# Spreading the decays of a state-space scan over the partitions: through memory with broadcast loads instead of TensorE transposes, and the block off the diagonal as a product with a cumulative product

## The reference

```python
xBC = jax.nn.silu(xBC_c.transpose(0, 2, 1) + conv_b)
...
dt = jax.nn.softplus(dt + dt_bias)
A = -jnp.exp(A_log)
...
decay = jnp.exp(dt * A)
dtx = dt[..., None] * xh

def step(h, inp):
    dec_t, dtx_t, B_t, C_t = inp
    h = dec_t[:, :, None, None] * h + dtx_t[..., None] * B_t[:, None, None, :]
    y_t = jnp.einsum('bhpn,bn->bhp', h, C_t)
    return (h, y_t)
```

## Time and profile before

| | us |
|---|---|
| median of 3 runs | 1030.62 |
| lowest, highest | 1022.71, 1031.51 |
| the profiled execution | 1024.98 |
| its span, first to last instruction | 1023.1 |
| mean granted clock of TensorE, as a share of 2.4 GHz | 0.945 |
| a full step of the first stage, steps 4 to 15 | 30.0 to 30.4 |

### The profile page before, as it was taken

How to read it: one execution, slowest core, us unless ns; L and a number is a source line. 1 busy time by engine, 2 the same in 40 slices (tenths; PEclk the granted TensorE clock), 3 DMA queues, 4 the chain that set the end, 5 groups by cost and what they waited for, 6 DMA issues and landing times.

```text
span 1023.1 us, 22359 instructions
## 1 busy us (share of the span) xinstructions
PE 905.9 (89%) x6324; PEld 790.4 (77%) x6325; DVE 724.6 (71%) x2092; ACT 502.3 (49%) x1259; POOL 587.5 (57%) x649
## 2 busy tenths in 40 slices
PE   4697999999999999999874369999999998669998
PEld 3576877877877787887654269999999998558887
DVE  5357799888889989888874335555555554599993
ACT  3333555554555555555322125555555554555653
POOL 5435455777778777777646454444444444365551
PEclk9989999999999999999966679999999999879999
DMA  7400000110100110000095112232221221224332
GB/s 180 90 11 11 1 11 12 31 31 22 30 17 27 32 31 27 16 19 16 18 275 158 40 44 68 78 85 67 65 67 55 58 64 54 56 81 114 97 101 51
DMA packets 72057, 59.12 MB, mean 58 GB/s; under 512 B 19169, under 2 KB 61468, under 8 KB 71985
## 3 DMA queue, kind: packets, MB, share of 16 engines
q1 hardware_dynamic: 63440, 41.88, 15.9%
q0 software_dynamic: 8544, 16.34, 4.8%
HBM read 35.62 MB, written 23.81 MB: 58 GB/s over the span
## 4 chain that ended last, share of the span: by engine, by line
PE 48%; DVE 24%; issue 15%; POOL 8%; another core or an unknown queue 1%; ACT 1%; DMA 1%; SPq 0%; DVEq 0%; POOLq 0%; ACTq 0%
PE psum L967 13%; PE psum L952 13%; DVE arena L1504 4%; DVE arena L1852 4%; PE psum L650 3%; POOL x_slots L1362 3%; PE psum L651 3%; PE psum L652 3%; PE psum L785 2%; PE psum L802 2%; DVE h_all L1552 2%; DVE arena L1857 2%; PE psum L961 2%; POOL arena L1338 2%; DVE arena L1512 2%
## 5 line engine op out<-in xcount | busy, mean ns | idle before, releaser
L1189 ACT ACTIVATE arena<-psum,arena 128x128 f32<-128x128 f32 x556 | 159.0, 369 | 155.9 <-PE psum L952 131.9
L1395 POOL DMA_INDIRECT y_tokens<-arena x139 | 136.8, 984 | 161.0 <-DVE arena L1802 117.1
L952 PE MATMUL psum<-arena 128*128 128x128 f32 x1112 | 154.5, 283 | 27.2 <-DVE arena L1795 15.7
L952 PEld LDWEIGHTS psum<-arena 128*128 128x128 f32 x1112 | 139.9, 198 | 29.1 <-DVE arena L1789 15.3
L967 PE MATMUL psum<-arena 128*128 x1112 | 156.4, 284 | 0.4 <-issue 0.4
L1362 POOL DMA_INDIRECT x_slots<-arena,idx x128 | 128.0, 1000 | 34.6 <-issue 34.3
L967 PEld LDWEIGHTS psum<-arena 128*128 128x128 f32 x1112 | 137.6, 194 | 7.4 <-issue 0.6
L1789 DVE COPY arena<-arena 128x644 f32 x139 | 75.4, 542 | 72.1 <-issue 65.6
L1795 DVE TENSOR_SCALAR arena<-psum,lng,lnb 128x128 f32<-128x128 f32 x139 | 56.9, 409 | 52.5 <-PE psum L961 40.8
L1504 DVE TENSOR_TENSOR_SCAN arena<-psum,arena 124x496 f32<-124x496 f32 x64 | 72.5, 1175 | 11.9 <-PE psum L785 7.8
L1332 POOL TENSOR_TENSOR arena<-arena 128x496 f32<-128x496 f32 x32 | 40.0, 1251 | 34.6 <-DVE arena L1532 34.6
(11 more groups left out here) (283 smaller groups left out, 2215.8 us busy)
## 6 DMA issues: line engine op xcount, KB each, us to landing
arena<-x_slots SPq DMA_DIRECT2D x139, 64.5 KB
arena<-y_tokens SPq DMA_DIRECT2D x16, 448.0 KB
arena<-in_x SPq DMA_DIRECT2D x16, 256.0 KB, 3.2
out_tokens<-arena SPq DMA_DIRECT2D x16, 224.0 KB
y_tokens<-arena POOLq DMA_INDIRECT x139
x_slots<-zero_src SPq DMA_DIRECT2D x33, 64.5 KB, 4.2
moe_all<-in_x SPq DMA_DIRECT2D x4, 512.0 KB, 5.8
x_slots<-arena,idx POOLq DMA_INDIRECT x128
```

The source lines that it names most:

```text
L952: last = nc.tensor.matmul(psum[:, 2 + b.q % 2, k * 128:(k + 1) * 128], w1_blk[b.q % 4][:, k * 128:(k + 1) * 128], hT[b.q % 2], start=True, ...
L1189: last = nc.scalar.activation(EHT[t.q % 2][:, k * 128:(k + 1) * 128], psum[:, 2 + t.q % 2, k * 128:(k + 1) * 128], ACT.Silu, bias=w1_blk[t ...
L1395: nc.gpsimd.indirect_dma_start(out=y_tokens, out_offset=bass.IndirectOffsetOnAxis(ap=xb[t.q][:, F:F + 1].bitcast(i32), axis=0), in_=YO[t.q ...
```

## The change

The decays take another way from GpSimd to the rows in every partition. In step b+1 TensorE transposes the 16 columns of a unit at once (`dec_rows(b, a)`, one transpose into [16 x 124] of bank 1), ScalarE copies the result twice to partitions 64 to 79 of the arena (`dec_copy`), once as it is and once with its first element kept, VectorE makes the cumulative products of the second copy (`cum_decays`, a scan over 16 partitions), SyncE stores both to memory (`decays_out`, four DMAs) and loads them back broadcast to 124 partitions (`decays_in`, two DMAs of 124 x 1488 numbers, one for each sequence). In the next step VectorE scans 992 numbers a sequence in place (`scans`), which gives the two blocks on the diagonal. The block off the diagonal is made without a scan: scores times the last column of the first block's scan times the cumulative product of the second block, four instructions a sequence (`decayed_scores`). `decays` on TensorE is gone, and `keep` with it.

Moved or rewired besides: on GpSimd `decay_of(b)` stands ahead of `add_bias(a)` and `gate(c,0)`; on VectorE `scans(c,1)` stands ahead of `skip_add(c,0)`, and `stats(a)` behind `cum_decays(b)`; on ScalarE `dec_copy(b)` stands ahead of `relu(a)`; the gate works in place, and the squares go to XT instead of a buffer of their own (so `silu(b,0)` waits for the row sums of the unit before the last, and two loads of expert weights wait for row sums instead of the gate); on SyncE the loads of x stand in turn with the new DMAs.

```diff
@@ memory and buffers
+    dec_rows_of = nc.dram_tensor("dec_rows_of", (2, 2, 12, CH), fp32, kind="Internal").ap()
...
-        L0 = take(CH, NH, L)
-        L1 = take(CH, NH, CH)
-        M0 = take(CH, NH, L)
-        M1 = take(CH, NH, CH)
-        Tg = take(128, 2, UT)
+        DB = [take(CH, 12, CH) for _ in range(2)]
+        M = take(CH, 3, NH, CH)
         Yg = take(128, 2, UT)
-        Sq = take(128, 2, UT)
+        diag8 = take(CH, 8, CH)
@@ SyncE
+                def decays_out(b):
+                    sp.wait_ge(S.cum_ready, b + 1)
+                    for n in range(2):
+                        later(sp, db_here[n], 16 * (b - 1))
+                    for n in range(2):
+                        sp.dma_start(dec_rows_of[b % 2, n, 0:8, :], dec_st[b % 2][8 * n:8 * n + 8, 0, :])\
+                            .then_inc(S.dec_stored, 16)
+                        sp.dma_start(dec_rows_of[b % 2, n, 8:12, :], dec_st[b % 2][8 * n + 4:8 * n + 8, 1, :])\
+                            .then_inc(S.dec_stored, 16)
+
+                def decays_in(b):
+                    sp.wait_ge(S.dec_stored, 64 * (b + 1))
+                    for n in range(2):
+                        later(sp, S.m_ready, 2 * (b - 1) + n + 1)
+                        sp.dma_start(DB[n].rearrange("p r t -> p (r t)"),
+                                     rows(dec_rows_of[b % 2, n].rearrange("r t -> (r t)"), CH)
+                                     .rearrange("p o t -> p (o t)"))\
+                            .then_inc(db_here[n], 16)
+
+                for t in range(UNITS + 1):
+                    if t + 2 < UNITS: load(t + 2)
+                    if t >= 1: decays_out(t - 1); decays_in(t - 1)
...
-                sp.wait_ge(S.yg_ready, 2 * UNITS - 2)
+                sp.wait_ge(S.pr_ready, UNITS - 1)
@@ TensorE
-                def decays(c, n):
...
-                    for h in range(NH):
-                        for k in range(2):
-                            col = (h % 2) * L + k * CH
-                            last = nc.tensor.transpose(psum[0:CH, 5 + h // 2, col:col + CH],
-                                                       dec[c % 2][:, 2 * n + k, h:h + 1].to_broadcast([CH, CH]),
-                                                       ident[0:CH, 0:CH])
-                    last.then_inc(S.pb_ready, 1)
+                def dec_rows(b, a):
+                    pe.wait_ge(S.dec_ready, b + 1)
+                    if a is not None:
+                        pe.wait_ge(S.tanh_done, a + 1)
+                    nc.tensor.transpose(psum[0:16, 1, 0:CH], dec[b % 2].rearrange("p j h -> p (j h)"),
+                                        ident[0:CH, 0:CH]).then_inc(S.dect_psum, 1)
...
-                    if c is not None: decays(c, 0); scores(c, 0)
+                    if c is not None: scores(c, 0)
...
-                    if c is not None: scores(c, 1); decays(c, 1)
+                    if c is not None: scores(c, 1)
...
                     if d is not None: logits(d)
+                    if b is not None: dec_rows(b, a)
                     if b is not None: projection(b, 1, None); projection(b, 2, None); x_rows(b)
@@ ScalarE
+                def dec_copy(b):
+                    act.wait_ge(S.dect_psum, b + 1)
+                    later(act, S.dec_stored, 64 * (b - 1))
+                    nc.scalar.activation(dec_st[b % 2][:, 1, :], psum[0:16, 1, 0:CH], ACT.Copy)
+                    nc.scalar.activation(dec_st[b % 2][:, 0, 1:], psum[0:16, 1, 1:CH], ACT.Copy)\
+                        .then_inc(S.dect_copied, 1)
...
-                    if a is not None: tanh(a); relu(a)
+                    if a is not None: tanh(a)
                     for n in parts_at(t): squares(n)
+                    if b is not None: dec_copy(b)
+                    if a is not None: relu(a)
@@ GpSimd
                 def decay_of(b):
                     pool.wait_ge(S.dt_ready, b + 1)
-                    later(pool, S.pb_ready, 2 * (b - 1))
+                    later(pool, S.dect_psum, b - 1)
                     link(pool, S.pool_link, nc.gpsimd.tensor_tensor(
                         dA, dt[b % 2], a_neg[:, :, :].rearrange("p j h -> p (j h)"), ALU.mult))
-                    link(pool, S.pool_link, nc.gpsimd.tensor_tensor(ee2, euler[0:CH, :], dA, ALU.pow))
-
-                    nc.gpsimd.tensor_tensor(dec[b % 2].rearrange("p j h -> p (j h)"), ee2, keep[:, :],
-                                            ALU.mult).then_inc(S.dec_ready, 1)
+                    nc.gpsimd.tensor_tensor(dec[b % 2].rearrange("p j h -> p (j h)"), euler[0:CH, :], dA, ALU.pow)\
+                        .then_inc(S.dec_ready, 1)
...
                     if v is not None and v < UNITS - 5: scatter(v, (2, 3))
+                    if b is not None: decay_of(b)
                     if a is not None: add_bias(a)
                     if c is not None: gate(c, 0)
-                    if b is not None: decay_of(b)
@@ VectorE
-                def long_scans(c, n):
-                    dve.wait_ge(S.pb_ready, 2 * c + n + 1)
...
-                def short_scans(c, n):
...
+                def scans(c, n):
+                    dve.wait_ge(db_here[n], 16 * (c + 1))
+                    o = DB[n][:, 0:8, :].rearrange("p r t -> p (r t)")
+                    V.tensor_tensor_scan(o, o, diag8.rearrange("p r t -> p (r t)"), 0.0, ALU.mult, ALU.add)\
+                        .then_inc(S.scan_done, 1)
...
-                    V.tensor_tensor(M0, L0, psum[0:CH, 4, 0:L].unsqueeze(1).broadcast_to([CH, NH, L]),
-                                    ALU.mult)
-                    V.tensor_tensor(M1, L1, psum[0:CH, 4, L:L + CH].unsqueeze(1)
-                                    .broadcast_to([CH, NH, CH]), ALU.mult).then_inc(S.m_ready, 1)
+                    G = psum[0:CH, 4, 0:3 * CH].rearrange("p (k t) -> p k t", t=CH)
+                    V.tensor_tensor(M[:, 0:3:2, :, :], DB[n][:, 0:8, :].rearrange("p (k h) t -> p k h t", h=NH),
+                                    G[:, 0:3:2, :].unsqueeze(2).broadcast_to([CH, 2, NH, CH]), ALU.mult)
+                    for h in range(NH):
+                        last = V.scalar_tensor_tensor(M[:, 1, h, :], G[:, 1, :], DB[n][:, h, CH - 1:CH],
+                                                      DB[n][:, 8 + h, :], ALU.mult, ALU.mult)
+                    last.then_inc(S.m_ready, 1)
+
+                def cum_decays(b):
+                    dve.wait_ge(S.dect_copied, b + 1)
+                    v = dec_st[b % 2][:, 1, :]
+                    V.tensor_tensor_scan(v, v, ones_col[64:80, :].to_broadcast([16, CH]), 1.0, ALU.mult, ALU.mult)\
+                        .then_inc(S.cum_ready, 1)
...
-                    if c is not None: long_scans(c, 0)
+                    if c is not None: scans(c, 0)
                     if b is not None: dt_first(b)
                     if a: x_rest(a)
-                    if c is not None: short_scans(c, 0); decayed_scores(c, 0)
+                    if c is not None: decayed_scores(c, 0)
...
-                    if c is not None: skip_add(c, 0); long_scans(c, 1); short_scans(c, 1); decayed_scores(c, 1)
-                    if a is not None: stats(a)
+                    if c is not None: scans(c, 1); skip_add(c, 0); decayed_scores(c, 1)
...
+                    if b is not None: cum_decays(b)
+                    if a is not None: stats(a)
                     if c is not None: skip_add(c, 1)
```

More of the change, by code:

```diff
@@ L269, in audio_tower @@
         pos[0] = 0
-        diag2 = take(CH, 2, L)
         w_out = take(128, 2, F)
@@ L318, in audio_tower @@
         dA = nab
-        ee2 = take(CH, 16)
+        pos[0] += 16
         free_at_gate = pos[0]
         Z, XT, BT, CT = [None] * 2, [None] * 2, [None] * 2, [None] * 2
+        dec_st = [None] * 2
         for q in (1, 0):
@@ L552, in _ @@
                         .then_inc(S.spare_filled, 16)
-                for u in range(2, UNITS):
-                    load(u)
+                def decays_out(b):
[18 more added lines that the diff above has]
+                    if t >= 1: decays_out(t - 1); decays_in(t - 1)
                 w1v = w1.rearrange("p (e h) -> p e h", e=E)
@@ L711, in dt_projection @@
                     later(pe, S.moe_ready, t - 3)
+                    later(pe, S.dect_copied, b)
                     for j in range(4):
@@ L750, in x_rows @@
                     pe.wait_ge(S.ip_used, 4 * b + 2)
-                    later(pe, S.scan_done, 2 * b)
+                    later(pe, S.xd_ready, b)
                     for j in range(4):
@@ L872, in shared_down @@
                         pe.wait_ge(S.table_ready, 1)
+                    if b is not None:
+                        pe.wait_ge(S.dect_copied, b + 1)
                     for j in range(4):
@@ L1079, in silu @@
                         later(act, S.yg_ready, 2 * (b - 1))
+                        later(act, S.pr_ready, b - 1)
                     what, part, bank = chunks[k]
@@ L1243, in _ @@
```

(6 more changed lines are left out.)

78 lines of the change are left out of this document (27 added, 51 removed).

## The result

The changed kernel takes 1113.95 us (median of 4 runs, 1109.8 to 1114.22); the kernel before took 1029.45 in the runs beside it. The ratio is 1.0824, with an interval of 1.0767 to 1.0881. I had forecast 1057 (1037 to 1080): slower was right, but the loss is 84 us, not 32.

A forecast was written before the change was run, and what follows sets the result against it. TensorE's ordered work and waits bound the kernel. On 1024.98 us: even steps 14.4, odd 9.0, steps 3 to 5 2.7, ends -4, clock 10.2, together +32.3, so 1057 us; range 1037 to 1080.

The forecast's parts named there:

- the bound: First stage, full steps of 30.0 to 30.4 us: TensorE's work in its order plus what it waits for.
- the place: Transpose L796, behind the logits and ahead of projection(b,1): TensorE waits 2 to 3 us in every step from 6.
- the releaser: GpSimd's power L1341, which makes the decays, ends TensorE's wait ahead of the new transpose L796.
- the clock: TensorE in steps 6 to 16: six of eleven gaps bring the clock down, 1.7 us each, +10.2 in all.
- one scan of 992 is priced the same: VectorE's long scans: 2.26 us for 992 numbers before, and the same price for the new single scan.
- steps 3 to 5: No scatter stands ahead and dt is the limit: projection 1.1, 1.1 and 0.5 us later, +2.7 together.
- the ends: Steps 1, 2 and the last, where VectorE or GpSimd sets the pace: 2 us for each of two steps, -4.
- Worth nothing: Removing decays(c,0) from TensorE, 0.97 us, gains nothing, since the scores behind it wait for mean_squares all the same.
- Rival (1): Load of the decays runs on few DMA engines and lands 1 to 4 us late: 1075 us, chance 0.16.
- Rivals (2): TensorE reaches the transpose late for another reason, half covering the wait: about 1.2 us a step, 1034, chance 0.12.
- (3): Decays arrive in time and TensorE has 0.89 us less to do in 14 steps: 1008 us, chance 0.07.
- `cum_decays` and the stores are hidden: Way through memory: stores land by 332.2 or 335.1, first sequence's load is hidden with 0.9 to 3.8 us to spare.

The follow-up runs named there:

- e6: e4 with eight identity transposes in place of four for the scans' diagonal; mean step 34.00 us, ratio 1.043 to the kernel before.
- e4: Changed kernel with the scans' diagonal written into PSUM by four TensorE transposes and each 992 scan cut into two of 496; step 33.40 us, ratio 1.035.
- e12: e6 with 12 useless matmuls on TensorE in the gap ahead of L796; mean step 32.33 us, ratio 1.033.
- e5: Changed kernel with eight useless identity transposes on TensorE ahead of scores(c,0); mean step 37.10 us, ratio 1.089.
- e9: Changed kernel with transpose behind x_rows, bias before decays, loads cut, PSUM diagonal by eight transposes, first square behind norm; step 29.91 us, ratio 0.996.
- e11: e9 with four transposes for the diagonal in place of eight; mean step 30.76 us, ratio 1.005.
- e10: e9 with each load of the decays in one piece of 124 rows; mean step 32.94 us, ratio 1.044.
- e2: Changed kernel with 20 useless matmuls on TensorE ahead of its wait for the decays; mean step 35.41 us, ratio 1.072.

## Why the prediction was right and wrong

**Right: the bound, the place and the releaser.** TensorE waits at L796 for GpSimd's power L1341 in each step, and the loss is in the steps. e6 is the kernel that I had described, and there my times hold: dt 9.2 us into the step (9.23 measured, in step 4), decays 13.85 in e4 (13.8), gap 2.83 and 2.79 us in even steps (2.7), 2.3 in odd ones (2.1). With the clock held (e12) a step is 2.26 us longer than before, where I had 2.13 on average (2.4 and 1.8).

**Wrong: the step that failed is "one scan of 992 is priced the same"**, with the gap worked out from GpSimd's old durations. The scan costs VectorE the same, 2.22 us; what I priced at nothing is that it now reads both inputs from SBUF and holds GpSimd meanwhile. It is worth 37.08 - 34.00 = 3.08 us a step, 34 of the 57 us that were missing (e6 against after; e5, with e6's eight transposes and the old scans, has 37.10, so it is the scans; e4 shows the held operations gone).

**Mis-sized: the clock.** A fall costs 1.67 us (I had 1.7), but there is one in each of the eleven steps instead of in six: 18.4 instead of 10.2. That gaps of 2.3 to 2.8 us suffice each time I could not know from two gaps of the trace; taking half of them was a guess between the bounds.

**Mis-sized: steps 3 to 5 and the ends.** The first lost 12.0 us, not 2.7. e6 loses 7.2 there, so 4.8 is held GpSimd. The other 4.5 can be the clock, which I had counted from step 6 on only: in e6 it is at 0.50 in each of these steps, until 107.5 us in step 3, then from 149 to 152 and 180 to 183, at waits of 1.44 us in step 4 and 0.92 in step 5; before, it was 1.00 there. At 1.67 us each that would be 5.0, an estimate. The ends came to 6.6 - 6.4 = +0.2 instead of -4: the last stretch gained as expected, but the first scan of all waited 5.3 us for its load, which I had not counted. The sum of these: 34 + 8 + 9 + 4, and 1.5 for the gap of the steps, is the 57 us between 32.3 and 89.3.

**"Worth nothing", for `decays(c,0)`.** In the changed kernel that is so (e5). Where the decays are not late it is not: there the eight transposes of e9 helped to hold the clock, and half of them gone costs 0.85 us a step (e11 against e9).

**Rival (1), the load binds,** did not happen: the scans of the changed kernel wait for memory in step 2 alone. The longer steps that late decays make can be one reason. But e12, with the same load and steps of 32.3 us, waits in steps 2 and 17 only. e10 has the transpose behind `x_rows`, some 2 us later, and steps that would be 29.9 us long without the load's waits (e9); there the load costs 48 us, and no run tells which of the two it takes. Rivals (2) and (3) had no part in it. That `cum_decays` and the stores are hidden was right.

## What to carry to other kernels

When a VectorE instruction changes where it reads from, look at what GpSimd does beside it: its duration on VectorE may stay to the hundredth and its price be elsewhere. Ask of every wait that a change adds in a tight order who comes late next if it is mended, and try the mends together: place alone gave 20 us, the scans alone 47, both with GpSimd's order and cut loads 75, and one square moved on ScalarE the rest. And of a transfer, count the DMA engines that its outer size lets it have before calling it hidden.

## What the runs showed of the hardware

- A scan of VectorE with both inputs in SBUF made a GpSimd operation of 0.19 us last 2.02, and a scatter 2.05 in place of 0.97; with one input in PSUM neither was touched.
- TensorE's granted clock fell to half at waits of 2.3 to 2.8 us in all ten steps from 6 to 15 of e6, behind 0.97 us in five of six cases (e11), behind 0.55 us in one of six (e9). At one of 2.20 us in e4 (step 12) it did not fall. So in this kernel the length of a wait alone did not decide it. After the falls at the transpose in the changed kernel and e6 it came back 3 to 6 us after TensorE was busy again, after the short waits of e9 and e11 7 to 8 us. One fall cost 1.67 us a step on average (e2 against the changed kernel, e12 against e6).
- A load to 124 rows moved at some 100 GB/s with a quarter of the DMA engines (e10); the same load cut into 112 and 12 rows reached 375 GB/s (e9).
